# Layer 3 of a four-layer kernel: the second normalisation of a batch done at the end of the stage of the batch before

## What is computed

```
xn = _layernorm(x, axis=-1)
x = x + _L2_attn_ref(xn, ...) + _L2_ffn_ref(xn, ...)

def _L2_attn_ref(x, norm1_w, norm1_b, norm2_w, norm2_b, ...):
    h = _layernorm(x, norm1_w, norm1_b)              # the second normalisation
    prev = jnp.pad(h[:, :-1], ((0, 0), (1, 0), (0, 0)))
    r = (h * time_mix_r + prev * (1.0 - time_mix_r)) @ Wr
    k = (h * time_mix_k + prev * (1.0 - time_mix_k)) @ Wk
    v = (h * time_mix_v + prev * (1.0 - time_mix_v)) @ Wv
    wkv = _wkv(r, k, v, time_decay, time_faaaa)
    x = x + wkv @ Wo
    h = _layernorm(x, norm2_w, norm2_b)              # the third
    prev = jnp.pad(h[:, :-1], ((0, 0), (1, 0), (0, 0)))
    mixed = h * cm_mix + prev * (1.0 - cm_mix)
    return x + sigmoid(mixed @ Wcr) * (relu(square(mixed @ Wck)) @ Wcv)

def _L2_ffn_ref(x, w_gate_up, w_proj):               # weights made ternary
    gate, up = jnp.split(x @ wq_gu.T, 2, axis=-1)
    h = silu(gate) * up
    return rms_norm(h) @ wq_p.T
```

## Time and profile before

| | us |
|---|---|
| median of 3 runs | 4454.59 |
| lowest and highest | 4450.3, 4455.68 |
| the profiled execution, its own time | 4455.64 |
| its span, first to last instruction | 4453.9 |

### The profile page before, as it was taken

The page is one execution under the profiler, slowest core; times in us unless marked ns, Lnnn a source line. Parts: engine busy times, 40 slices in busy tenths (PEclk is TensorE's granted clock), DMA queues, the critical chain, the costliest instruction groups (busy, mean ns, idle before and its releaser), DMA issues. The chain is left out here.

```text
span 4453.9 us, 60802 instructions
## 1 busy us (share of the span) xinstructions
PE 3618.9 (81%) x22476; PEld 2148.0 (48%) x22476; DVE 2582.3 (58%) x5398; ACT 1795.4 (40%) x2662; POOL 708.1 (16%) x890
## 2 busy tenths in 40 slices
PE   6887878887578788887866788887988988898897
PEld 3434244342435436354354556655653653663672
DVE  6757667675664644545446445354765665664764
ACT  2362634627163553635413343343035126216206
POOL 3111121111100100001002232131311210220220
PEclk8998989989789899898987898988999999999999
DMA  5414224041400000000010000002000000000000
GB/s 188 129 34 132 64 81 134 29 147 49 153 1 1 29 1 29 1 1 29 1 64 19 29 1 29 29 1 78 1 1 29 1 1 29 1 1 29 1 1 11
DMA packets 147078, 176.98 MB, mean 40 GB/s; under 512 B 16384, under 2 KB 123392, under 8 KB 146688
## 3 DMA queue, kind: packets, MB, share of 16 engines
q1 hardware_dynamic: 138320, 153.03, 10.9%
q0 software_dynamic: 6144, 16.79, 1.1%
q10 hardware_dynamic: 2320, 3.28, 0.2%
HBM read 126.40 MB, written 51.38 MB: 40 GB/s over the span
## 5 line engine op out<-in xcount | busy, mean ns | idle before, releaser
L691 DVE TENSOR_REDUCE arena<-ps 128x2 f32<-128x1024 f32 (+3 forms) x768 | 697.1, 952 | 108.3 <-PE ps L659 97.8
L889 ACT ACTIVATE arena<-ps 128x1024 f32<-128x1024 f32 (+3 forms) x768 | 575.3, 812 | 108.3 <-PE ps L796 104.0
L972 DVE TENSOR_TENSOR arena<-arena,tri 128x256 f32<-128x256 f32 x512 | 209.8, 423 | 299.4 <-ACT arena L889 295.4
L796 PE MATMUL ps<-arena 64*128 64x512 f16 (+3 forms) x1536 | 257.3, 349 | 122.3 <-ACT arena L889 80.8
L448 PE MATMUL ps<-arena,xn_t 128*128 128x512 f32 (+1 forms) x768 | 299.8, 543 | 65.9 <-PEq L65 46.4
L813 PE MATMUL ps<-arena 128*17 128x512 f32 (+3 forms) x3072 | 341.2, 518 | 6.4 <-DVE arena L972 4.0
L889 ACT ACTIVATE attention<-ps 128x1024 f32<-128x1024 f32 (+3 forms) x384 | 287.9, 809 | 131.3 <-PE ps L796 131.2
L2357 ACT ACTIVATE arena<-ps 128x256 f32<-128x256 f32 x192 | 63.6, 381 | 621.9 <-PE ps L2299 575.6
L796 PEld LDWEIGHTS ps<-arena 64*128 64x128 f16 x1536 | 70.9, 94 | 469.7 <-ACT arena L889 379.9
L813 PE MATMUL ps<-attention 128*33 128x512 f32 (+3 forms) x1536 | 289.2, 500 | 0.0
L659 PE MATMUL ps<-arena 64*128 64x512 f16 (+3 forms) x1536 | 233.1, 330 | 31.0 <-DVE arena L691 30.1
(11 more groups left out here) (317 smaller groups left out, 6673.4 us busy)
## 6 DMA issues: line engine op xcount, KB each, us to landing
arena<-w_experts SPq DMA_DIRECT2D x128, 256.0 KB, 3.3
acc<-sums SPq DMA_DIRECT2D x16, 1024.0 KB, 5.9
x_next<-sums SPq DMA_DIRECT2D x16, 1024.0 KB, 8.4
arena<-slots_x SPq DMA_DIRECT2D x32, 512.0 KB, 4.7
slots_y<-arena SPq DMA_DIRECT2D x32, 512.0 KB, 4.3
sums<-acc SPq DMA_DIRECT2D x24, 512.0 KB, 2.9
making<-basis SPq DMA_DIRECT2D x16, 768.0 KB, 5.4
slots_x<-arena SPq DMA_DIRECT2D x1, 4096.0 KB, 28.2
```

Source lines behind the costliest of these rows:

```text
L691: dve.reduce_max(a.mp[:, 2 * j:2 * j + 2, qt, c], out[:, :, 0:w], AX.X).then_inc(self.pair_out, 1)
L796: last = pe.matmul(m.ps[:, 4 + 2 * (v % 2) + odd, q0:CH], a.k[half, pair, kt * P:(kt + 1) * P], a.q[half, pair, c * CH + q0:(c + 1) * CH], ...
L889: act.activation(a.p[:, v % ring, :, q0:CH], m.ps[:, b:b + 2, q0:CH], ACT.Exp, scale=HD ** -0.5).then_inc(exped, 1)
L972: dve.tensor_tensor(diag, diag, keep, ALU.min).then_inc(masked, 1)
```

## The change

mixing_layer gets two more arguments: begun (true for batches 1 to 3) and begin (true for batches 0 to 2). Where begin is true, a third Normalisation, `coming`, is done at the end of the stage for the next batch, from m.xn and into m.x (as scratch) and f.h_t. Where begun is true, `second` is left out. Seven semaphores more are in each stage (60). Where begun is true, the first calls of the engines are also in another order: project(0) ahead of ffn_up(3); silu(2) and split(2) ahead of keep_k; mix(0) ahead of join(0).

```diff
 class Normalisation:
+    def vector_stats(self, dve, t):
+        if self.ready is not None:
+            dve.wait_ge(self.ready, t + 1)
+        dve.bn_stats(self.st[:, t, :], self.src[:, t, :]).then_inc(self.stats, 1)
+
     def vector(self, dve):
+        for t in range(NT):
+            self.vector_stats(dve, t)
+        self.vector_scale(dve)
+
+    def vector_scale(self, dve):
         src = self.src
-        for t in range(NT):
-            if self.ready is not None:
-                dve.wait_ge(self.ready, t + 1)
-            dve.bn_stats(self.st[:, t, :], src[:, t, :]).then_inc(self.stats, 1)
...
     def scalar(self, act):
-        m = self.m
+        self.scalar_root(act)
+        self.scalar_store(act)
+
+    def scalar_root(self, act):
         act.wait_ge(self.std_in, NT + 1)
         act.activation(self.std, self.veps, ACT.Sqrt).then_inc(self.std_done, 1)
+
+    def scalar_store(self, act):
+        m = self.m
...
-def mixing_layer(nc, m, f, w, wg, wu, wd, batch, fetch, store):
+def mixing_layer(nc, m, f, w, wg, wu, wd, batch, fetch, store, begun, begin):
...
+        coming = Normalisation(m, m.xn, m.x, f.h_t[:, :, 1:S + 1], norm_sems[2 * n_norm:3 * n_norm], w.n1w, w.n1b, place=1)
+        ahead = NextNormalisation(m, norm_sems[3 * n_norm:])
...
                 for j in range(TC):
+                    if c == 1 and j == TC // 2 and begin:
+                        pe.wait_ge(ahead.kept, NT // 2)
+                        pe.wait_ge(scaled, NT)
+                        coming.tensor(pe)
                     terms = [(i, q) for i in range(ni) for q in range(2)]
...
             ffn_up(0)
             ffn_up(1)
-            second.tensor(pe)
+            if not begun:
+                second.tensor(pe)
             ffn_up(2)
-            ffn_up(3)
+            if not begun:
+                ffn_up(3)
             project(0)
+            if begun:
+                ffn_up(3)
             ffn_up(4)
...
             split_x(0)
-            second.scalar(act)
+            if not begun:
+                second.scalar(act)
             silu(0)
             silu(1)
             split_x(1)
             split(0)
             split(1)
+            if begun:
+                silu(2)
+                split(2)
             for u in range(4):
                 keep_k(u)
-            silu(2)
+            if not begun:
+                silu(2)
             silu(3)
-            split(2)
+            if not begun:
+                split(2)
             split(3)
...
             for i in (14, 15):
                 silu(i)
                 split(i)
+            if begin:
+                coming.scalar_root(act)
             roots(1)
+            if begin:
+                coming.scalar_store(act)
...
-            second.vector(dve)
-            join(0)
-            dve.wait_ge(second.stored, NT // 2)
+            if not begun:
+                second.vector(dve)
+                join(0)
+                dve.wait_ge(second.stored, NT // 2)
             dve.wait_ge(first_column, 1)
             mix(0)
+            if begun:
+                join(0)
             join(1)
...
                 if 2 <= t < 2 + NT // 2:
                     ahead.vector_keep(dve, t - 2, 6 + t % 2)
+                if begin:
+                    coming.vector_stats(dve, t)
+            if begin:
+                dve.wait_ge(ahead.kept, NT // 2)
+                coming.vector_scale(dve)
             mean_squares(1)
             ffn_add(1)
...
-                    mixing_layer(nc, m, f, w, wgu[:, :, 0:F1], wgu[:, :, F1:2 * F1], wp, b, into[2], into[3])
+                    mixing_layer(nc, m, f, w, wgu[:, :, 0:F1], wgu[:, :, F1:2 * F1], wp, b, into[2], into[3], b > 0, b + 1 < B)
```

3 lines of the change are left out of this document (1 added, 2 removed).

## The result

| | us |
|---|---|
| the changed kernel, median of 4 runs | 4405.54 (4400.37 to 4407.67) |
| the kernel before, median of 4 runs beside it | 4452.44 (4446.93 to 4455.68) |
| ratio | 0.9891, 95% interval 0.9879 to 0.9904 |
| predicted | 4418, range 4410 to 4431 |

The profiled execution took 4406.35 us, its span 4404.6, so 49.3 less than the span of before.

The account below looks back on a forecast made before the run. The stage start was taken as bound by the second normalisation's chain, not TensorE's work. 4455.64 - 44.0 (front) + 5.7 (turns) + 1.6 (semaphore clears) = 4419, or 4418 against the median; range 4410 to 4431.

Parts of the forecast that it names:

- The front: Start of the stage in batches 1 to 3, up to ffn_up(6): 14.65 us less a batch, 44.0 in all.
- steps 2 to 5: TensorE's layout from ffn_up(0) to project(1): no waits, project(0) from +12.6, joins and keep_k in time by 1.4 and 1.7.
- step 1: Stage start: mix(0) on VectorE and GpSimd's x_low hinder each other, TensorE begins at +4.25, 1.0 us late a batch.
- what was called hidden: Stage end, batches 0 to 2: bn_stats, VectorE's chain, square root and 8 activations cost nothing while ffn_down(1) runs.
- The turns: 16 turns on TensorE between the halves of ffn_down(1): 1.91 us each time, no wait, 1.0 to spare.
- the clears: SyncE clears 7 more semaphores in each of four stages, 0.058 us each, 1.6 us in all.
- nothing won: Rival at 4457, chance 0.03: mix(0) or join(0) still waits as late as before, so only the costs remain.
- more won: Rival at 4411, chance 0.12: no hindrance at the stage start (3.0), and better clock (4 more over three batches).
- The queue rival: Rival at 4429, chance 0.15: the join(2) and keep_k chain slips, TensorE stands about 3.5 before project(1), 10.5 in all.
- The turns did not wait: Denies the rival at 4426, chance 0.05: VectorE's chain 3.5 late, TensorE waits at the turns, 2.5 a batch.
- The slow rival: Rival at 4495, chance 0.03: TensorE's clock stays low until project(2) ends, costing 25.5 a batch, 40 slower in all.

Follow-up runs that it names:

- e4: Changed kernel with only the normalisation moved, first calls of batches 1 to 3 in their old order; 4421.99 us, ratio 0.9931 to the kernel before.
- e3: Changed kernel, with VectorE waiting for GpSimd's two x_low subtractions before mix(0) in batches 1 to 3; 4403.01 us, ratio 0.9890 to the kernel before.
- e9: Kernel before, with 7 idle semaphores more in each of the third layer's four stages; ratio 1.0004 to the kernel before.
- e11: Changed kernel, with the 7 more semaphores in batch 0's stage alone; ratio 0.9903 to the kernel before.
- e13: Changed kernel, with 8 idle semaphores more in the first stage of each fourth-layer batch; ratio 0.9918 to the kernel before.
- e14: Kernel before, with 8 idle semaphores more in the first stage of each fourth-layer batch; ratio 1.0011 to the kernel before.
- e2: Changed kernel run again without an edit; ratio 0.9897 to the kernel before.
- e15: Changed kernel, with a useless block of one 864-element tensor_reduce between the third and fourth layers; ratio 0.9907 to the kernel before.
- e5: Kernel before, with a useless block of one 64-element tensor_reduce between the third and fourth layers; ratio 1.0001 to the kernel before.
- e7: Kernel before, with a useless block of two 832-element tensor_reduces between the third and fourth layers; ratio 1.0007 to the kernel before.
- e1: Kernel before run again without an edit; ratio 0.9999 to the kernel before.

## Why the prediction was right and wrong

**Right: the bound and the mechanism.** The start of the stage was set by the moved chain and by the order of the first calls. Laid out anew, it came as written, TensorE's start within 0.02 and out(0) within 0.4. The front gave 44.9 for 44.0. e4 showed that the order of the first calls carries 9 of them, as steps 2 to 5 rested on it.

**Right: the hindrance of VectorE and GpSimd, step 1.** 1.0 us at TensorE's start, in the trace (2.17 and 3.49) and shown by e3, which took it away. What it was said to cost the kernel, 3 us, is not shown: without it batches 1 to 3 were 1.6 us shorter on one pair of traces and 5.2 on another, and no difference is clear of the noise in total time.

**Right: what was called hidden.** The last bn_stats, the chain, the square root and the 8 activations stay inside the wait for ffn_down(1). The spare time was larger than thought for the turns: the first is not before 2525.96, when 6 of 8 tiles are scaled. The turns cost 1.66 each time, not 1.91: the prediction took the row's busy time for the price, and not the time to the next start. That is 0.75 of the miss.

**Right: the clears.** 60 clears take 3.4 us in batch 0's boundary where 53 took 3.0, and e9 has the same. The third layer of e9 was 7.4 longer, not 1.6; the difference is in part batch 0's own variation, and 3.5 of it stays without a cause. In e11 21 clears fewer made the third layer no shorter.

**Wrong, without effect: the price of "nothing won".** By the prediction's own costs, 4454.6 + 5.7 + 1.6, that rival stands at 4462, not 4457.

**Wrong: the sum took all that lies outside the front as unchanged.** That is the step that failed: 4455.64 - 44.0 + 5.7 + 1.6 has no term for TensorE's clock in stretches whose work doesn't change but whose pauses end at another moment. Behind out(0), the third layer's stages 1 to 3 are 2.3 us shorter in all than the turns and clears allow. In batch 1, 32 matmuls of out(t) took 9.65 us before and 8.86 after. Windows over their first 9.7 us, before and after:

```profile
2598.40:2608.10 9.70, 9.70 (x35) 8.19 (x35) 3.50 (x9) 2.43 (x3) 5.83 (x5) 0.74 0.01 2
```

```profile
2584.20:2593.90 9.70, 9.70 (x41) 8.33 (x42) 4.29 (x11) 2.44 (x3) 5.83 (x5) 0.82 0.00 0
```

TensorE pauses 3.9 us ahead of them in both, but the granted clock behind the pause is 0.82 instead of 0.74. In the fourth layer it is 7.3 us, the largest term of the miss, and there the prediction had no term at all. The way from the edit to it is: seven semaphores more in each stage of the third layer are 28 instructions more on SyncE, so the longer gap falls out of the boundaries of batches 2 and 3, TensorE's pauses there are 4.3 instead of 4.7 us, and its clock is back about 3 us sooner. e13 and e14, which made the pauses 4.7 or more in both kernels, took the difference away. In batch 1 the pause is 4.3 in both kernels and the changed one is still 3.4 us shorter; the boundary ahead of it has the longer gap in the kernel before alone. Batch 0 goes the other way, by 3.2. The clock had a place in it, twice: as "more won", with up to 4 us over three batches, and as a slower rival within the front. Both looked at stretches that the change touches. But in the fourth layer a stretch behind a pause gained or lost some 3 us of high clock when the pause ended 0.46 us sooner or later, and the change moves every later pause of the kernel.

**The accounts.** Forecast 36.6 less. Measured between the traces 49.3: the front 0.9 better, the turns 0.75 better, the clock in the third layer some 2.3 better, the fourth layer 7.3 better, the first two layers 1.5 better, which differ by more than that between traces of one kernel, and batch 0 of the third layer 0.3 worse. These make 12.5 of 12.7. The medians beside each other differ by 46.9 and, in the second comparison, by 45.7, so some 2 to 4 of the 49.3 belong to the two profiled executions. Of the 12.5 us between 4418 and 4405.54, 2.2 are that the kernel before came out at 4452.44 beside it, not at the 4454.59 that the forecast started from. In e2 the changed kernel took 4409.35, 0.65 below the range. So how far the time missed the range is in part luck; that the gain was too small in the forecast, by about 10 us, is not.

**The rivals.** The queue rival did not come: no wait ahead of project(1). The turns did not wait. The slow rival (clock low through project(2)) fell: over the 10 us from 2551 on the granted clock is 1.00, and over +4 to +38 it is 0.92.

```profile
2541.00:2551.00 10.00, 8.84 (x26) 6.86 (x27) 5.29 (x6) 2.95 (x6) 1.22 (x2) 0.67 0.50 171
2551.00:2561.00 10.00, 10.00 (x32) 5.80 (x31) 9.82 (x8) 5.54 (x11) 9.16 (x5) 1.00 0.00 0
```

"More won" comes nearest, but for the smaller part of its reasons. The hindrance came, so its 3.0 did not. The clock gave 2.3 us in the third layer, where up to 4 were allowed, and 7.3 in the fourth, which this rival doesn't name. It stood at 4411, and with the range closed at 4410 what came was shut out; a term of some 5 us either way for the clock in unchanged layers would just have held the time.

**Left open.** Why the clock comes back after 3 us in one batch with a short pause and after 6 in another: e15 shows the late return with a short pause and no longer gap ahead of the batch, and e5 to e7 and e15 moved it with a delay of 0.4 to 2.0 us ahead of the layer, but also with 3 instructions more on SyncE. The place of arrival that gives the one or the other was not found. The longer gap on SyncE comes every 128 recorded instructions; what SyncE does in it no trace shows.

## What to carry to other kernels

When a chain of small steps at a stage's start holds the main engine, and the stage before ends with that engine busy and the others idle, moving the chain there and putting the main engine's free work first can be sized well by laying the queues out step by step with the row's times, start to start. Then add a term for TensorE's clock wherever TensorE pauses, in code that is not touched too: here 7 of 49 us came from there. A comparison of two versions within 0.2% says little on an edit. Compare the stage that was edited, in more than one trace, and look how much a stage that wasn't edited differs between them: here up to 6.6 us in batch 0 of the third layer.

## What the runs showed of the hardware

- After a pause at which TensorE's clock fell to 1.2 GHz, resuming 0.46 us later cost a batch about 3.5 us (e13: 344.1 to 344.9 became 347.4 to 348.9 in three batches). In 48 batches of the fourth layer the clock was back either 2.8 to 3.1 or 5.7 to 6.2 us after TensorE resumed, and the batch took 343.6 to 345.0 or 347.3 to 349.0 accordingly. The pattern is the same in a repeat of the same program (e1, e2), so a few microseconds in unchanged code are reproducible and still no property of the code.
- SyncE clears one semaphore per 0.058 us, and at some boundaries the run of clears is 0.4 to 0.5 us longer (2.0 instead of 1.5 for 28, 3.7 instead of 3.4 for 60). It is one gap of 0.37 to 0.45 us, and it stands behind every 128th instruction that the trace records on SyncE, in all 86 places of 17 traces where that instruction and the next are clears.
- A function table's load on ScalarE starts ahead of the wait of the activation that needs it (2539.08 against 2545.97).
